# Sums over the partitions moved from the matmul engine to a chain of accumulating DMAs, and compressed inputs loaded once per batch

## The reference, cut to what matters

```python
c_q = h @ w_down_q.T                    # compressed, 128 wide
c_kv = h @ w_down_kv.T
q = (c_q @ w_up_q.T).reshape(b, s, H, DH).transpose(0, 2, 1, 3)   # H = 16 heads of DH = 64
k = (c_kv @ w_up_k.T)...; v = (c_kv @ w_up_v.T)...
q, k = rope(q), rope(k)
attn = softmax(einsum('bhqd,bhkd->bhqk', q, k) / 8)
out = einsum('bhqk,bhkd->bhqd', attn, v)
```

## Time and profile before

| | us |
|---|---|
| median of 3 runs | 3598.4 (3596.11 to 3598.8) |
| the profiled execution, its own time | 3596.49 |
| its span | 3594.9 |
| busy in it: PE, DVE, ACT, POOL | 3542.5, 3041.8, 2741.8, 1275.9 |

### The profile page before, as it was taken

The page is one execution under the profiler, slowest core; times in us unless marked ns, Lnnn a source line. Parts: engine busy times, 40 slices in busy tenths (PEclk is TensorE's granted clock), DMA queues, the critical chain, the costliest instruction groups (busy, mean ns, idle before and its releaser), DMA issues. The chain is left out here.

```text
span 3594.9 us, 79981 instructions
## 1 busy us (share of the span) xinstructions
PE 3542.5 (99%) x24458; PEld 2368.6 (66%) x24458; DVE 3041.8 (85%) x4214; ACT 2741.8 (76%) x3888; POOL 1275.9 (35%) x1304
## 2 busy tenths in 40 slices
PE   6999999999999999999999999999999999999999
PEld 5755555555555555555555555554799999999999
DVE  8878888888888888888888888888777777777799
ACT  5778888888888888888888888888666666666665
POOL 2213232222232323232323232332566666666400
PEclk9999999999999999999999999999999999999999
DMA  7987989898989898989898989896666665666797
GB/s 261 360 295 172 216 194 215 193 216 193 215 195 215 194 215 195 214 196 213 197 211 199 211 199 209 200 210 142 227 213 223 211 226 211 223 212 227 238 370 272
DMA packets 541990, 790.89 MB, mean 220 GB/s; under 512 B 253725, under 2 KB 401310, under 8 KB 505824
## 3 DMA queue, kind: packets, MB, share of 16 engines
q0 software_dynamic: 101648, 406.73, 46.5%
q1 hardware_dynamic: 440272, 383.30, 36.2%
HBM read 453.60 MB, written 138.81 MB: 165 GB/s over the span
## 5 line engine op out<-in xcount | busy, mean ns | idle before, releaser
L1238 ACT ACTIVATE at_ex<-at_st 128x1024 f32<-128x1024 f32 x1024 | 1048.0, 1024 | 217.7 <-PE at_st L1377 214.2
L1435 PE MATMUL at_pv<-at_ex,at_v 128*64 128x512 f32 x4096 | 991.6, 605 | 0.0
L1081 DVE TENSOR_REDUCE at_mx<-at_fr 128x1 fp32r<-128x512 f32 x1024 | 704.3, 688 | 298.6 <-PE at_fr L1445 273.3
L1262 ACT ACTIVATE at_fr<-at_fr 128x512 f32<-128x512 f32 x1024 | 605.4, 591 | 124.7 <-PE at_fr L1445 105.4
L1435 PEld LDWEIGHTS at_pv<-at_ex,at_v 128*64 128x64 f32 x4096 | 248.2, 136 | 504.4 <-issue 504.4
L1377 PE MATMUL at_st<-at_qh,at_kh 64*128 64x512 f32 x2048 | 500.4, 391 | 1.8 <-DMA at_top<-at_mx 1.6
L1377 PE MATMUL at_st<-at_qh,at_kl 64*128 64x512 f32 x2048 | 499.9, 390 | 0.0
L1377 PE MATMUL at_st<-at_ql,at_kh 64*128 64x512 f32 x2048 | 498.5, 389 | 0.0
L1442 PEld LDWEIGHTS at_fr<-at_kdif,at_qh 64*128 64x128 f32 x1024 | 187.9, 183 | 417.3 <-issue 310.6
L1445 PE MATMUL at_fr<-at_kfar,at_qh 64*128 64x512 f32 x1024 | 455.6, 445 | 5.3 <-DVE at_mx L1081 4.3
L1442 PE MATMUL at_fr<-at_kdif,at_qh 64*128 64x512 f32 x1024 | 454.5, 444 | 1.8 <-DVE at_mx L1081 0.9
(11 more groups left out here) (213 smaller groups left out, 6249.2 us busy)
## 6 DMA issues: line engine op xcount, KB each, us to landing
at_cq<-scr_c SPq DMA_DIRECT2D x62, 1024.0 KB, 6.8
at_ck<-scr_c SPq DMA_DIRECT2D x62, 1024.0 KB, 5.7
at_sum<-at_ex POOLq DMA_DIRECT2D x95, 512.0 KB, 5.9
at_sum<-at_sum POOLq DMA_DIRECT2D x95, 512.0 KB, 6.1
scr_v<-pj_v SPq DMA_DIRECT2D x64, 512.0 KB, 6.9
at_v<-scr_v SPq DMA_DIRECT2D x64, 512.0 KB, 7.4
mid_rec<-scr_rec SPq DMA_DIRECT2D x256, 128.0 KB
scr_o<-mid_oT SPq DMA_DIRECT2D x64, 512.0 KB
```

The costliest lines, as they stand in the source:

```text
L1081: e.reduce_max(mx[k // QB][:, h * QB + k % QB:h * QB + k % QB + 1], fr[h][:, :], AX.X).then_inc(s_tr[h], 1)
L1238: e.activation(ex[k][:, :, :], st[u % 2][:, :, :], ACT.Exp, scale=SCALE).then_inc(s_exp, 1)
L1262: e.activation(fr[h][:, :], fr[h][:, :], ACT.Relu).then_inc(s_pos[h], 1)
L1435: mm = e.matmul(pv[n][rows[h], :], v[i.u][:, kt, rows[h]], ex[kt][:, h, :], start=(kt == 0), stop=(kt == KT - 1))
```

## The change

- `denominators` leaves PE in the steady part. The joined sums of two halves stand in one buffer `total` (half 0 of pair i with half 1 of pair i-1), and GpSimd's queue folds its 128 partitions onto one with seven accumulating DMAs, each adding the upper half of the remaining partitions to the lower: 64 rows of 8 KB, then 32, 16, 8, 4, 2, 1. Each waits until the one before has landed. They stand between the other DMAs of that queue (below).
- `spread` reads the one row that is left. It waits for the seventh fold, stands one `max_row` earlier than before, and `recip` moves from group 7 to group 5, `gather` and both `each` into the same pair's body. ACT's copy is gone.
- `add_keys` waits, for its first addition of half 1, until that same pair's `spread` has landed, since it writes where `spread` reads.
- The 1 MB loads of compressed input happen for the first pair of each batch alone; for the others the semaphore is raised without a load.
- The last pairs (`ahead` < 2) keep PE's products, now in group 2, and the tail is reordered.

```diff
@@ sync
+                if j.off % HP == 0:
+                    load_c(j, x)
+                else:
+                    e.sem_inc(s_ld[x][j.u], 16)
...
+            def spread(i):
+                wait_apart(e, s_recc, i.n(1, -1), s_apart_s)
+                wait_apart(e, s_fold_sum, i.n(16 * FOLDS), s_apart_s)
+                for n in (0, 1) if prior(i) else (0,):
+                    for h in range(2):
+                        e.dma_start(denc[:, h, n, :], total[1 - i.u][0:1, n, h, :].rearrange("o (p k) -> o p k", p=P)).then_inc(s_denc, 16)
...
                     max_row(one, 1, 1)
+                if prev and ahead >= 2:
+                    spread(i)
...
+                if ahead:
                     max_row(one, 2, 0)
+                    max_row(one, 2, 1)
+                    max_row(one, 3, 0)
                 if prev:
-                    spread(prev, (0, 1))
+                    gather(i, (0, 1) if prior(i) else (0,))
                 if ahead:
+                    max_row(one, 3, 1)
+                    max_row(one, 4, 0)
+                if prev:
+                    if prior(i):
+                        each(i, 1)
+                    each(i, 0)
+                if ahead:
+                    max_row(one, 4, 1)
                     max_row(one, 5, 0)
+                if prev and prior(i):
+                    store(prev.next(-1))
@@ gpsimd
+            def fold_sums(i, k):
+                half = P >> (k + 1)
+                if k:
+                    wait_apart(e, s_fold_sum, i.n(16 * FOLDS, 16 * k), s_apart)
+                else:
+                    wait(e, s_one[1], i.n(32))
+                    wait_apart(e, s_one[0], i.n(32, 32), s_apart)
+                ns = slice(0, NH2) if prior(i.next(1)) else slice(0, 1)
+                e.dma_start(total[i.u][0:half, ns, :, :], total[i.u][half:2 * half, ns, :, :], accum_op=ALU.add).then_inc(s_fold_sum, 16)
@@ gpsimd, body: the order of the queue (folding: ahead >= 2)
+                    fold_sums(prev, 2)
                     add_sums(prev, 1)
+                    fold_sums(prev, 3)
+                    fold_sums(prev, 4)
                     add_sent(i, 0)
+                    fold_sums(prev, 5)
+                    fold_sums(prev, 6)
                     add_swapped(i.next(2), Q)
                     add_sums(i, 0)
                     add_swapped(i.next(2), K)
+                if ahead >= 3:
+                    fold_sums(i, 0)
                     add_sent(i, 1)
+                    place_copies(i.next(d))
+                if ahead >= 3:
+                    fold_sums(i, 1)
+                    place(i.next(d))
@@ vector, add_keys (first addition of a half) and body
-                    wait(e, s_df, i.n(1, n - 1))
+                    wait(e, s_denc, i.n(64, 64 * n - 96))
...
+                    if g == 5 and prev:
+                        recip(i, slice(0, 2 if prior(i) else 1))
-                    if g == 7 and prev:
-                        recip(prev)
@@ scalar, tensor
-                    if g == 4 and prev:
-                        den_copy(prev, 1)
+                    if g == 2 and ahead < 2:
+                        den_copy(i, 1, 0, 2 - ahead)
-                    if g == 4 and prev:
...
-                        denominators(prev)
+                    if g == 2 and ahead < 2:
+                        e.wait_ge(s_osb, i.n(2, 0))
+                        denominators(i)
```

More of the change, by code:

```diff
@@ L736, in attend_parts @@
         ADDED = (1, 1, 2, None, 3, 3, 4, 5)
-        c, cos, sin, raw, sums = (below[n] for n in ("c", "cos", "sin", "raw", "sums"))
+        FOLDS = 7
+        c, cos, sin, raw, late_sum = (below[n] for n in ("c", "cos", "sin", "raw", "late"))
         swp = [sb(f"swp{x}", [P, S]) for x in "qk"]
@@ L797, in rotated, with prior, joined @@
                 e.wait_ge(s_rot[x], j.n(32))
+        def prior(i):
+            return not (isinstance(i.n(), int) and i.n() < 2)
+        def joined(j, n):
+            return total[j.u if n == 0 else 1 - j.u][:, n, :, :]
         def slot_of(i, g):
@@ L813, in run, with run_batches @@
                     i = At(it, off)
+                    body(i, i.next(-1), 4)
+            for n in range(NPAIR - 5, NPAIR):
+                i = At(0, n)
+                body(i, i.next(-1), NPAIR - 1 - n)
+            tail(At(0, NPAIR - 1))
+        def run_batches(e, prologue, body, tail):
+            prologue()
+            for n in range(3):
+                i = At(0, n)
+                body(i, i.next(-1) if n else None, 4)
+            with e.Fori(0, NBATCH - 1) as it:
+                for off in range(3, 3 + HP):
+                    i = At(it * (HP // 2), off)
                     body(i, i.next(-1), 4)
@@ L930, in body @@
                     max_row(one, 1, 1)
+                if prev and ahead >= 2:
+                    spread(i)
+                elif prev:
+                    spread_rows(i, (0, 1), 0, 2 - ahead)
+                if ahead:
                     max_row(one, 2, 0)
+                    max_row(one, 2, 1)
+                    max_row(one, 3, 0)
                 if prev:
-                    spread(prev, (0, 1))
+                    gather(i, (0, 1) if prior(i) else (0,))
                 if ahead:
[L935 to L938, removed]
+                    max_row(one, 3, 1)
[6 more added lines that the diff above has]
+                    max_row(one, 4, 1)
                     max_row(one, 5, 0)
[L940 to L943, removed]
+                if prev and prior(i):
+                    store(prev.next(-1))
             def tail(i):
-                for n in range(NH2):
-                    each(i.next(-1), n)
-                spread(i, (0,))
-                store(i.next(-1))
[L950 to L954, removed]
+                end = i.next(1)
+                spread_rows(end, (0, 1), 0, 3)
+                gather(end)
+                each(end, 1)
+                each(end, 0)
+                store(i.next(-1))
+                spread_rows(i.next(2), (1,), 1, 4)
+                gather(i.next(2), (1,))
+                each(i.next(2), 1, 32 * NPAIR)
                 store(i)
@@ L1208, in tail @@
                     add_keys(i, n, k)
-                for n in range(NH2):
-                    normalise(i.next(-1), n)
-                recip(i, slice(0, 1))
+                normalise(i.next(-1), 0)
+                recip(i.next(1))
             run(e, prologue, body, tail)
@@ L1218, in after @@
                 if g == 0:
+                    normalise(last.next(-1), 1)
                     normalise(last, 0)
-                    recip(last, slice(1, 2), 1)
+                    recip(last.next(2), slice(1, 2), 64 * NPAIR)
                 if g == 1:
@@ L2329, in build @@
                 "raw": [asb(f"raw{x}", [P, S]) for x in "qk"],
-                "sums": [[[asb(f"sum{n}{a}", [P, 2, HALF])] * 2 for a in range(2)] for n in range(NH2)],
+                "late": [asb(f"late{n}", [P, 2, HALF]) for n in range(NH2)],
+                "total": asb("total0", [P, NH2, 2, HALF]),
             }
```

114 lines of the change are left out of this document (57 added, 57 removed).

## The result

The changed kernel takes 4480.6 us (median of 4 runs, 4477.2 to 4483.8) beside 3598.6 us (3596.1 to 3599.4): a ratio of 1.2451, 95% interval [1.2435, 1.2467]. The profiled execution took 4483.8, its span is 4481.3. The prediction had the direction, with 3700 and a high end of 3810; the time is 671 us above that end. A pair takes 50.4 us on the mean, where 37.65 were forecast and 35.9 were taken before. That is from the instructions of `spread` in the folded pairs: 61 times from 305.4 to about 3328 us (the fourth of the last one starts at 3331.3).

What follows compares the result with a forecast made beforehand. PE was taken as the bound. Losing its products saves 1.00 us per pair, but waits of 2.35 and 0.4 make 37.65 instead of 35.9: 105 us over about 60 pairs, forecast 3700, range 3532 to 3810 (own range 3635 to 3770).

Steps and rivals of the forecast that it cites:

- The term for `spread`, 6.1 us: SP's four DMAs after fold 6: last issued 2.7 us after the first, landed 3.4 later, at +37.65 against +34.9.
- What bounds the kernel before, the products: Attention stage: PE full; removing its products of ones saves 1.00 us per pair, leaving 34.9 us if nothing waits.
- GpSimd's queue "looks free": GpSimd idles 4.9, 5.0, 6.7 and 1.0 us before DMAs until DVE is ready, so seven new waits go there.
- the rival of 0.17: Small `spread` and `gather` pieces queue behind large accumulating DMAs: 40 us per pair or more, 3800 to 3950; chance 0.17.
- The place and the kind of wait: DVE idles before half 1's first addition until a DMA into `mid_denc` lands; PE idles before `step_y`, waiting 2.35 us.
- `add_sums(prev, 1)` is issued at +15.4. It cannot be earlier: In GpSimd's queue, this DMA follows DVE's last addition of the pair and starts the late folds, 15.4 us after *a*.
- second chain: Reciprocal, `gather`, `each`, then DVE's `normalise` in group 7 at +11.5: DVE 1.85 us late, PE waits about 0.4 us.
- a: Start of DVE's first addition of half 1, at 1027.47; the forecast's + times count from it.
- Folds 0 to 2 have been issued by then ... taken at 0: First three folds in GpSimd's queue are issued before `add_sums(prev, 1)`, with about 1 us of room; cost 0.
- Landing of 512 KB, 5.0 us: `add_sums(prev, 1)` and `add_sent(i, 0)` each delay the fold behind them; 5.0 us without loads, 6.1 measured with them.
- The loads go: cost both at nothing: Compressed-input loads of 2 MB go for 7 of 8 pairs, folds add 1016 KB per pair; neither costs bandwidth.
- The high bound: Slow landings, `spread` in 7 us and 1.0 for the broadcast wait give 42.0 us per pair; end taken as 3810.

Runs made afterwards that it cites:

- three folds and both moves: Changed kernel without folds 3 to 6 (copy for reciprocal), half 1's multiplication in the next pair's group 0, `spread` four `max_row`s earlier in SP's queue: 3650.3 us.
- folds_beside: Kernel before, compressed input loaded once per batch, plus seven chained accumulating DMAs per pair on a zero buffer with 4 KB rows, unawaited by other engines: 3696.7 us.
- late_quiet: Changed kernel, all seven folds; GpSimd waits behind fold 6 for `spread` to land, and half 1's multiplication moves to the next pair's group 0: 4514.2 us.
- late_half: Changed kernel, all seven folds, with the multiplication of half 1 moved to group 0 of the next pair: 4389.2 us.
- warm_full: Changed kernel with 40 added matmuls of zeros with 128 rows per pair on PE, before the step that waits for DVE in group 6: 4463.0 us.
- quiet_spread: Changed kernel with GpSimd waiting behind fold 6 until `spread` has landed, before it issues the swaps and `add_sums(i, 0)`: 4480.0 us.
- c_once: Kernel before with the compressed input loaded once per batch, products of ones staying on PE: 3597.6 us, ratio 0.9999.
- warm: Changed kernel with 40 added matmuls of zeros with 32 rows per pair on PE, where it waits for DVE in group 6: 4608.7 us.

## Why the prediction was wrong, step by step

Two steps failed. The term for `spread`, 6.1 us, was mis-sized: it was 12.6. And GpSimd's queue, taken as free, was not: the prediction counted it only from `add_sums(prev, 1)` to fold 6 and put all else in it at nothing. The direction was right, and by the wait that was forecast, not by luck; the rest follows term by term.

- **What bounds the kernel before, the products:** right as far as tested. With three folds and both moves PE is back at 386 of 400 us. That a pair free of waits takes 34.9 us was not reached by any kernel (36.8 at best), so this term isn't shown.
- **GpSimd's queue "looks free":** wrong. It was idle because it waited for DVE, and that idle time isn't room for dependent landings. In `folds_beside` the queue alone takes 37.3 us from one fold 6 to the next, with half the bytes; in `late_quiet`, where it never stands waiting for DVE, a pair takes 51.0. The chance for this ("each landing is as before") lay in the rival of 0.17.
- **The place and the kind of wait:** right. DVE stands before the first addition of half 1, PE in front of `step_y` (now L1511), and `mid_denc` ends it.
- **"`add_sums(prev, 1)` is issued at +15.4. It cannot be earlier":** it was later, +18.7. I took the start as given and wrote the second chain as a loss of 0.4 us for PE, beside the first. But `normalise` stands on DVE between *a* and that DMA, so its wait lies inside the first chain. The second chain itself took 13.3 us from *a* instead of 11.5. `late_half` takes its wait away, gains 1.2 us there and 91 us in all, and leaves +17.5. The 2.1 us that stay over 15.4 are those by which PE, stopped and started again at the low clock, makes DVE's third reduction late (+8.1 beside +6.0): a term that the prediction didn't have at all. With the clock kept up they go, but the wait for the broadcast takes them over (`warm_full`).
- **"Folds 0 to 2 have been issued by then ... taken at 0":** held in the changed kernel, where `add_sums(prev, 1)` waits for DVE (4.55 us) and not for a fold. It had only 5 us to give: in `quiet_spread` the folds hold it back, to +25.8.
- **Landing of 512 KB, 5.0 us:** too short. From `add_sums(prev, 1)` to fold 4 it is 7.5 us (1540.11 to 1547.58; the sum has 6.3), from fold 4 to fold 5, with `add_sent` between, 4.7 (3.3). Then 3.55 to fold 6 (3.9) and 2.6 to `spread` (2.65). Together the chain from `add_sums(prev, 1)` to `spread` is 18.4 instead of 16.15. The 6.1 us of the earlier trace rows were at hand, and `c_once` shows that removing the loads doesn't shorten them. With 6.1 that first leg would have come to 7.4.
- **`spread`, 6.1 us:** the largest miss, 12.6. I took the row near the kernel's end, where nothing lay beside it, and did not ask what GpSimd issues right behind fold 6: two swaps, `add_sums(i, 0)` and two more swaps, 1.5 MB in all. The prediction put such queueing into the rival "everything heavy", priced it at 3800 to 3950 and gave it 0.17. `quiet_spread` shows what that company costs `spread`, 4.0 against 12.6. It doesn't follow that the 8.6 us could be had: with `spread` at 3.9 to 4.0 the pairs of `quiet_spread` and `late_quiet` still took 50 and 51 us, since the queue that had been held back was full.
- **"The loads go: cost both at nothing":** true of the kernel before, wrong in the changed one, where having them back costs 293 us. A load hidden under a full PE isn't hidden from a chain of DMAs.
- **The high bound:** I took 42.0 per pair, some 3962 us, and then cut it to 3810, "since PE's waiting empties the DMA engines". Uncut it would have been 518 us short as well. They did get idler (0.70 on average), but not in the moment that counts: in the 6 us from the issue of `spread` they are 0.97 busy. An average of a stage says nothing of a burst.

```profile
1508.00:1514.00 6.00, 4.43 (x26) 1.97 (x24) 2.48 (x4) 3.95 (x6) 3.32 (x4) 1.00 0.97 173
```

- **The circle:** `add_keys` waits for `spread`, the late sums wait for `add_keys`, the folds for the late sums, `spread` for the folds. The sum does go from one *a* to the next, so it has this circle; what it lacks are the waits of DVE inside it, for the broadcast and for PE. In such a loop each us on the path counts once per pair (`late_half`), unless a wait beside it ends no earlier (`warm_full`).
- **The rule against the sum.** The Trainium skill, DMA: Bandwidth & Descriptors, "Anatomy of one DMA — SWDGE (gpsimd) path", would have the chain in time. The runs disagree: 512 KB accumulated land in 5.8 to 6.1 us (`c_once`, beside the other traffic of that kernel), and from fold 5, of 16 KB, to fold 6 it is 3.6 us in the changed kernel.

No version that was run beats the kernel before; `c_once` equals it. Three kernels that would tell more were not run: one with a third buffer for the sums, so that DVE needn't wait for `spread`; the change with the multiplication moved and PE's clock kept up together; and the seven folds with the swaps left out. So what the seven folds cost at the least stays open.

## What to carry to other kernels

When a change puts a chain of DMAs on a buffer that is used in the same pair, close the circle on paper: go round once from the wait to itself, and count every wait of every engine on the way, also one that looks like another chain's. Then do the same for the in-order queue that the chain stands in. Price a small DMA by what is issued into the engines around it, not by its own bytes or by a quiet stretch of the trace. An idle in-order queue is no free place for dependent DMAs: count the landings in it, here 3.6 us for a small one and 5 to 7 behind 512 KB.

## What the runs showed of the hardware

- Four DMAs of 2 KB in 16-byte pieces took 4.0 us to the instruction that waits when GpSimd's queue was held back (`quiet_spread`), and 12.6 us beside 1.5 MB of accumulating DMAs from that queue (the changed kernel).
- A small dependent accumulating DMA costs 3.6 us from its issue to that of the next (16 KB: 1552.31, 1555.86), and 2.6 to SP's next start for the last, of 8 KB (1555.86, 1558.48).
- The granted clock fell to 0.50 under 40 matmuls with 32 rows (`warm`) and stayed at 1.00 under 40 with 128 rows (`warm_full`), in the same place, both back to back.
- Keeping the clock up made DVE's reduction behind the wait 2.5 us earlier and the pair only 0.3 us shorter, since DVE then waited 2.1 us longer for the broadcast.
